# Decoder of two layers, one core: the last step of the sixth norm moved from VectorE to ScalarE, between two pairs of root instructions

## The reference, cut to what matters

```python
x = _layernorm(x + _L0_attn_ref(x, ...))          # random features        -> norm 1
x = _layernorm(x + _L0_xattn_ref(x, ctx, ctx,..)) # cross attention        -> norm 2
x = _layernorm(x + _L0_ffn_ref(x, ...))           # gated rotation, 3 cycles-> norm 3
x = _layernorm(x + _L1_attn_ref(x, ...))          # state space scan       -> norm 4
x = _layernorm(x + _L1_xattn_ref(x, ctx, ctx,..)) # gated unit on ctx      -> norm 5
x = _layernorm(x + _L1_ffn_ref(x, ...))           # 8 experts, top 1       -> norm 6
# _layernorm(x) = (x - mean) / sqrt(var + 1e-5), over the 256 features
```

## Time and profile before

| | us |
|---|---|
| median of 3 runs | 3106.39 |
| lowest, highest | 3101.62, 3107.36 |
| the profiled execution's own time | 3099.29 |
| its span, first to last instruction | 3097.5 |
| PE, DVE, ACT, POOL busy | 2540.1, 2495.3, 1727.8, 1487.4 |
| mean granted TensorE clock | 0.872 |

### The profile page before, as it was taken

The page is one execution under the profiler, slowest core; times in us unless marked ns, Lnnn a source line. Parts: engine busy times, 40 slices in busy tenths (PEclk is TensorE's granted clock), DMA queues, the critical chain, the costliest instruction groups (busy, mean ns, idle before and its releaser), DMA issues.

```text
span 3097.5 us, 41602 instructions
## 1 busy us (share of the span) xinstructions
PE 2540.1 (82%) x11020; PEld 1469.9 (47%) x11020; DVE 2495.3 (81%) x4288; ACT 1727.8 (56%) x3062; POOL 1487.4 (48%) x1159
## 2 busy tenths in 40 slices
PE   6896888979888897888988788888888889887556
PEld 3544554544444454445545444554544445454323
DVE  2368888897978889898888978788897888978783
ACT  1457564646657474665646466564656646465620
POOL 1046354554535455563545545354553545456460
PEclk7868888888989989999898899898898989978687
DMA  3000000000000000000000000000000000000000
GB/s 131 10 8 10 14 11 14 17 14 7 10 21 10 14 17 14 7 10 21 10 14 13 18 7 10 21 10 14 13 3 21 10 14 7 7 7 1 14 7 7
DMA packets 16849, 45.72 MB, mean 15 GB/s; under 512 B 2248, under 2 KB 7056, under 8 KB 16400
## 3 DMA queue, kind: packets, MB, share of 16 engines
q1 hardware_dynamic: 16656, 43.96, 4.2%
HBM read 35.57 MB, written 8.39 MB: 14 GB/s over the span
## 4 chain that ended last, share of the span: by engine, by line
PE 47%; DVE 28%; issue 14%; ACT 7%; DVEq 2%; POOL 1%; ACTq 0%; DMA 0%; SPq 0%; POOLq 0%
PE bank L535 45%; DVE h_ring L1087 14%; DVE x L1199 3%; DVE ln_stats L387 2%; DVE smax L991 1%; POOL ysum L1671 1%; ACT a_ring L1479 1%; DVE x L405 1%; DVE xpad L1093 1%; PE bank L413 1%; DVE soft L1066 1%; ACT L1485 1%; ACT L1339 1%; DVE ln_mv L391 1%; ACT spare L1420 1%
## 5 line engine op out<-in xcount | busy, mean ns | idle before, releaser
L1671 POOL TENSOR_TENSOR ysum<-ysum,h_ring 128x512 f32<-128x512 f32 x896 | 1155.2, 1289 | 633.3 <-DVE h_ring L1087 571.3
L1087 DVE TENSOR_TENSOR_SCAN h_ring<-a_ring,bank 128x512 f32<-128x512 f32 x1024 | 1172.7, 1200 | 27.2 <-ACT bank L1474 16.2
L1479 ACT ACTIVATE a_ring<-soft,decay 128x510 f32<-128x510 f32 x1024 | 675.7, 717 | 198.4 <-DVE h_ring L1087 198.0
L535 PE MATMUL bank<-w_expert_w,x45T 128*128 128x512 f32 x1024 | 541.1, 675 | 199.0 <-DVE x L1199 191.4
L535 PEld LDWEIGHTS bank<-w_expert_w,x45T 128*128 128x128 f32 x1024 | 213.2, 216 | 490.9 <-DVE x L1199 253.5
L1658 POOL TENSOR_TENSOR soft<-xc,soft 128x512 f32<-128x512 f32 x64 | 81.0, 1276 | 655.2 <-ACT soft L1457 655.2
L535 PE MATMUL bank<-x3T,w_winT 128*128 128x512 f32 x512 | 291.0, 704 | 39.7 <-ACT x3T L419 31.4
L991 DVE TENSOR_REDUCE smax<-bank 128x4 f32<-128x480 f32 x256 | 156.4, 652 | 143.1 <-PE bank L535 143.1
L535 PE MATMUL bank<-qT,kmask 32*120 32x256 f32 x1024 | 207.2, 497 | 50.2 <-ACT spare L1386 40.6
L535 PE MATMUL bank<-spare,w_cn_w 128*128 128x256 f32 x768 | 217.7, 408 | 37.0 <-ACT spare L1416 22.4
L1199 DVE SCALAR_TENSOR_TENSOR x<-bank,weight,x 128x256 f32<-128x256 f32 x512 | 212.5, 474 | 40.4 <-PE bank L535 40.4
(11 more groups left out here) (149 smaller groups left out, 3890.2 us busy)
## 6 DMA issues: line engine op xcount, KB each, us to landing
x0T<-in_xT SPq DMA_DIRECT2D x16, 512.0 KB, 3.3
x<-in_x SPq DMA_DIRECT2D x16, 512.0 KB, 4.3
out<-x SPq DMA_DIRECT2D x16, 512.0 KB, 3.0
ctxT<-in_ctxT SPq DMA_DIRECT2D x16, 240.0 KB, 2.5
ctxTb<-in_ctxT SPq DMA_DIRECT2D x16, 240.0 KB, 2.7
ctxb<-in_ctx SPq DMA_DIRECT2D x16, 240.0 KB, 3.0
w_expert_w<-in_expert_w SPq DMA_DIRECT2D x1, 2048.0 KB
w_winT<-in_winT SPq DMA_DIRECT2D x1, 1024.0 KB
```

The source lines that it names most:

```text
L535: return pe.matmul(o, l, r, start=start, stop=stop)
L1087: scanned.then(v.tensor_tensor_scan(h_ring[:, k % HRING, :], a_ring[:, k % RING, :, :].rearrange("p b s -> p (b s)"), xc2, 0.0, ALU.mult, ...
L1479: a.activation(a_ring[:, k % RING, :, 1:S], delta[:, c, :].rearrange("p (b s) -> p b s", b=NB)[:, :, 1:S], ACT.Exp, scale=decay[:, k:k + 1 ...
L1671: p.tensor_tensor(out=total, in0=first, in1=h_ring[:, k % HRING, :], op=ALU.add)\
```

## The change

The apply of norm 6 leaves DVE. DVE computes instead a column of four biases, -mean times root (`ln6_shift`, one `scalar_tensor_tensor` of 128 by 4), between `rotate(f, 4)` and `rotate(f, 5)`. ACT takes the roots of norm 6 ahead of those of norm 3, waits for the bias column, and applies norm 6 with four activations (Identity, bias and scale from columns), 128 by 256 each; the roots of norm 3 come last. One semaphore and one small buffer are new.

```diff
+        shift6 = sb("shift6", [P, NT])
...
+        shift6_ready = sem("shift6_ready", 1)
...
         @block.vector
-            def ln6_apply(g):
+            def ln6_shift(g):
                 n = n6
                 v.wait_ge(n.rstd_ready.sem, n.rstd_ready.at(g, 1))
-                for t in range(NT):
-                    v.tensor_scalar(n.x[:, t, :], acc[:, t, :], n.mv[:, t, 0:1], n.rstd[:, t:t + 1],
-                                    ALU.subtract, ALU.mult).then_inc(n.x_ready.sem, 1)
+                v.scalar_tensor_tensor(out=shift6[:, :], in0=n.mv[:, :, 0], scalar=-1.0, in1=n.rstd[:, :],
+                                       op0=ALU.mult, op1=ALU.mult).then_inc(shift6_ready.sem, 1)
...
                 if f is not None:
                     rotate(f, 4)
+                if b is not None:
+                    ln6_shift(b)
+                if f is not None:
                     rotate(f, 5)
...
                     norm_apply(v, n3, f)
-                if b is not None:
-                    ln6_apply(b)
...
         @block.scalar
+            def ln6_apply(g):
+                n = n6
+                a.wait_ge(shift6_ready.sem, shift6_ready.at(g, 1))
+                for t in range(NT):
+                    a.activation(n.x[:, t, :], acc[:, t, :], ACT.Identity, bias=shift6[:, t:t + 1],
+                                 scale=n.rstd[:, t:t + 1]).then_inc(n.x_ready.sem, 1)
...
                 if nxt is not None:
                     norm_rstd(a, n1, nxt)
+                if b is not None:
+                    norm_rstd(a, n6, b)
+                    ln6_apply(b)
                 if f is not None:
                     norm_rstd(a, n3, f)
-                if b is not None:
-                    norm_rstd(a, n6, b)
```

## The result

The changed kernel took 3121.96 us (median of 5 runs, 3113.51 to 3123.58), the kernel before 3104.67 on the same chip (5 runs, 3099.73 to 3107.36): ratio 1.0053, 95% interval 1.0038 to 1.0068. Slower, by about 17 us; forecast was 4 us less. Run again in a later job it gave 1.0051 (1.0034 to 1.0069; label a0_after_again).

A forecast was written before the change was run, and what follows sets the result against it. The prediction saw the chain held at each loop jump by ScalarE's stops, counted from its jump, ahead of TensorE's long run. -5.0 at 12 jumps and +0.6 at the end gave -4.4: 3102.0 us, range 3093 to 3112.

The forecast's parts named there:

- TensorE's clock blurs this: At the 12 jumps, the shift could turn seams fast or slow, about 1.5 us each; likeliest case 3096 to 3108.
- Rival (b): TensorE idles less, so three of six slow mamba_in starts turn fast or half fast: -8.9 us, 3097.5; chance 14%.
- Part 6: SyncE's store and x load go out earlier, the load during ScalarE's two stops; taken as 0.
- Rival (d): The x load hinders ScalarE's restart, stops growing by d = 0.95 us each jump: +7.0 us, 3113; chance 9%.
- Part 4: Norm 3's roots last before ScalarE's jump: jump and copies 0.42 us earlier, stops unchanged, 12 jumps, -5.0 us.
- Part 1: Four instructions, 1.39 us a turn, leave VectorE, which then only waits longer for xpad: worth 0.
- Part 2: Bias column on VectorE between the rotations: a 0.09 us slot hidden by norm 3's sum waiting for TensorE; cost 0.
- Part 3: Four activations on ScalarE, 1.9 to 2.2 us, hidden in its 10.49 us of idleness; cost 0.
- Part 5: End of the program: column, hand over and four activations replace norm 6's apply on VectorE: +0.6 us, bounds +0.3 and +1.2.

The follow-up runs named there:

- e1: Kernel before with only the two pairs of roots swapped on ScalarE, norm 6's ahead of norm 3's: 3113.9 us, ratio 1.0041.
- g2: Kernel before with three added ScalarE activations behind the last roots, each waited out: 3131.2 us, ratio 1.0100.
- e8: Kernel before with four added ScalarE activations behind the last roots, none waited for: 3103.7 us, ratio 1.0024.
- e5: Kernel before with 12 extra unused matmuls a turn in TensorE's waits near the seam: 3087.7 us, ratio 0.9964.
- e2: Changed kernel with SyncE's x load put behind the two context loads, so issued late: 3114.5 us, ratio 1.0054 to the kernel before.
- e3: Kernel before with SyncE's x load issued early, ahead of the norm 6 store: 3124.1 us, ratio 1.0085.
- g1: Kernel before with one added ScalarE activation behind the last roots, waited out: 3116.6 us, ratio 1.0052.
- g4: e10 with 20 more extra matmuls among the experts: 3062.4 us, ratio 0.9878 to the kernel before.
- e10: Kernel before with the roots swapped on ScalarE and 18 extra unused matmuls a turn: 3060.8 us, ratio 0.9877.
- e7: Kernel before with the roots swapped on ScalarE and 12 extra unused matmuls a turn: 3072.6 us, ratio 0.9923.
- e9: Kernel before with 12 extra matmuls and an unused column instruction on VectorE between rotations 4 and 5: 3087.5 us, ratio 0.9952.
- e6: Changed kernel with the x load behind the context loads and 12 extra matmuls: 3077.8 us, ratio 0.9929 to the kernel before.
- g3: Changed kernel with the x load behind the context loads and 18 extra matmuls: 3067.6 us, ratio 0.9891 to the kernel before.
- e11: Kernel before with the x load issued ahead of the store and 12 extra matmuls: 3094.9 us, ratio 0.9990.

## Why the prediction was wrong

The forecast was 3102.0, in 3093 to 3112; it came out at 3121.96, outside the range and on the other side.

**The step that failed** is "TensorE's clock blurs this", with its "A shift of 0.42 us can move a turn from one kind to the other either way". I took the clock as noise around the sum, 3096 to 3108, as if each seam fell for itself. The turns are not independent: turns of 184.3 us, with the clock low at the same places, follow one another, in one pattern six times in e1, in another 12 of 12 times in g2. How a turn hands its pattern to the next was not tested. The kernel before had 2 such turns of 12, and most shifts made them more: 0.28 us earlier, 0.46 later and 1.08 later all lose, and only the 0.06 of e8 can't be told from no change. Rival (b), fewer slow starts, had the same cause and the wrong sign: 11 slow seams, not 3.

How much is clock? Time at 1.2 GHz follows from the page, 2 x (1 - clock) x span: 793 us before, 859 after, 846 in e1, 713 in e5. The spans are 14.2 and 13.5 us longer for 66 and 53 us more of it, and e5's is 22.8 shorter for 80 less: 0.2 to 0.3 us of span for each. The runs say the same: among those of the kernel before, a run with 1 us more at 1.2 GHz is 0.23 to 0.37 us longer in the four later jobs (16 to 27 runs each, correlation 0.70 to 0.86). Of after's 14.2 the seam's 12 x 0.24 = 2.9 and the end's 0.9 leave about 10 for the clock.

As an estimate, 12 times the shift of `mamba_in` and 0.29 us for each microsecond at 1.2 GHz (means of all runs) give +10 for e1, +11 for e2, +28 for e3, +8 for e8, +18 for a0, +18 for g1 and +38 for g2 (e2 and a0 with the end's 0.9); their mean times differ from that of before by +12, +15, +25, +5, +18, +16 and +32. It fails for g4, where it gives 16 less than e10 and nothing is won. This division is worked out, not measured; that the clock makes the sign is shown by e1 and e7.

**Part 6**, "I take 0; the price is a rival's", failed too. Rival (d) at 9% was true as a mechanism: the stop grew by 0.53, and with the 0.14 of stop 1 that is d = 0.67 against a lead of 0.42, so `mamba_in` should be 0.25 later, and is 0.24 later. My argument against it, that 512 KB are through in 1.7 us, gave no protection: the restart of ScalarE suffered all the same. Its own size, d = 0.95, was too large. Rival (d)'s formula, with the measured d, gives 12 x 0.25 + 0.6 = 3.6 us, not 17. So the forecast had the seam's sign wrong by leaving d out, the rival had it right, and both missed the rest; that the rival's 3113 lies nearest to the result is luck.

**Part 4** was right in its direction and too large in the seam: 0.28 of 0.42 in e1, since I held the first stop constant and it went from 2.76 to 2.90. That the stop is counted from ScalarE's own jump, and not from PE's data, is borne out by e1 and g2: the copies move with the last Exp. The Trainium skill, "Runtime: NRT & Kernel Launch", section "Instruction fetch mechanics", has a taken branch whose target is out of the pages at hand fetch it by DMA before it goes on. The trace agrees: an instruction packet follows the last Exp by 0.97 to 1.01 us at the 12 jumps of before, none does at the exit, and the second stop grows while another load is in flight (0.52 before, 1.09 in e3).

**Part 1**: right, no gain. VectorE waits 4.81 us for xpad in the turn shown, over the 3 that were forecast, and 70.2 us in all for 16 times where it was 52.7.

**Part 2**: the slot of 0.07 to 0.09 and its cover are right; norm 3's sum waits 0.12 to 0.13 in the tight turns where it waited 0.19 to 0.23, as forecast. Only three of the changed kernel's 14 turns are of that kind, where ten were; in the others the sum waits 1.8 us or more. e9 prices the column at nothing.

**Part 3**: hidden as forecast. The activations last 0.59 us on average and 2.08 for four, inside the 1.9 to 2.2. The 400 ns worked out for one of them was too low, and so was the 0.1 to 0.2 us by which the four would be longer than VectorE's 1.38: it is 0.7.

**Part 5**: +0.9 for the forecast +0.6, within its bounds. The last statistics end at 3105.70 and the last activation at 3108.57, 2.87 us; before it was 1.98 (0.60 of waiting and the apply's 1.38). The row:

```profile
3106.50 2.07 ACT L1500 ACTIVATE x<-x,shift,ln_rstd 128x256 f32<-128x256 f32 x4 [0.23 <-DVE shift L1222]
```

## What to carry to other kernels

Where a kernel repeats a turn and the granted clock falls in it, first look whether the low stretches lie in the same places turn after turn; if they do, a shift of 0.3 us can cost (as here) several tenths of a per cent, and the sum of the terms is better tested with the clock held up, with a look at whether it is then equal outside the seam too. Holding it up was worth more here than the change under study: 18 small matmuls in TensorE's waits and the roots swapped gave 1.2%. And when an instruction that a queue waits for moves earlier, ask what the transfer behind it now meets: a load in flight at an engine's jump cost that engine half a microsecond.

## What was not expected of the hardware

- ScalarE's second stop after a jump, 0.52 us where the 512 KB load goes out only at its end and 0.53 to 0.59 where it goes out long after (e2, e6, g3), was 0.99 to 1.22 on average with the load in flight from the first stop on, in five profiles of four kernels, and up to 1.9 (e11). In g1 and g2, where ScalarE comes later and the load does not, it was 0.62 and 0.77. Whether the other engines' jumps suffer likewise was not looked at.
- The first stop is not constant: 2.76 us in the kernel before and 2.75 to 2.84 in the others with both pairs of roots at the end and no waited activation, 2.89 to 2.93 where one pair stands last, but 2.83 in g4. What makes the difference is open.
- Four activations that nothing waits for, issued just before the jump, delay it by 0.06 us; one that is waited out, by 0.37 (stop 1 of 3.13 against 2.76).
- A whole loop can run for 12 turns in the same 184.3 us pattern of granted clock (g2), and there are two such patterns of one length (g2, e1). Why the kernel before mostly stays out of it, and whether a better pattern than its own two turns of 177.9 and 180.6 can be had without filler, stays open.
